# Eight PSUM banks for the node update, its bias in three batches, and fifty unread products on TensorE

## The reference

```python
features = x[src]                                             # 200000 x 64
Y = relu(concat([features, edge_attr], axis=1) @ M_W.T + M_b)
Z = segment_sum(Y, dst, num_segments=6250)
h = relu(concat([x, Z], axis=1) @ U_W.T + U_b)
out = layernorm(x + h)                                        # over 64 features, eps 1e-5
```

## Time and profile before

| | us |
|---|---|
| median of 3 runs (1639.28 to 1639.89) | 1639.65 |
| profiled execution, its own time | 1641.58 |
| its span, first to last instruction | 1639.7 |
| busy: TensorE, VectorE, GpSimd, ScalarE | 1596.5, 1332.8, 1223.9, 347.5 |

### The profile page before, as it was taken

How to read it: one execution, slowest core, us unless ns; L and a number is a source line. 1 busy time by engine, 2 the same in 40 slices (tenths; PEclk the granted TensorE clock), 3 DMA queues, 4 the chain that set the end, 5 groups by cost and what they waited for, 6 DMA issues and landing times.

```text
span 1639.7 us, 53864 instructions
## 1 busy us (share of the span) xinstructions
PE 1596.5 (97%) x18182; PEld 1542.8 (94%) x18182; DVE 1332.8 (81%) x1391; ACT 347.5 (21%) x661; POOL 1223.9 (75%) x1303
## 2 busy tenths in 40 slices
PE   5899999999999999999999999999999999999996
PEld 5899999999999999999999999999999999999995
DVE  6788887888887888888888788888788878878874
ACT  4431111212112112211211111211221211212111
POOL 6777777777777777777777777777777777777774
PEclk9999999999999999999999999999999999999998
DMA  8333332323333333333333333323333332323222
GB/s 176 71 72 72 70 79 65 80 64 79 66 79 65 76 75 71 73 66 79 69 74 72 71 73 72 74 69 73 71 72 78 67 78 65 80 65 78 66 59 47
DMA packets 177806, 120.89 MB, mean 74 GB/s; under 512 B 107140, under 2 KB 156018, under 8 KB 177528
## 3 DMA queue, kind: packets, MB, share of 16 engines
q0 software_dynamic: 40992, 42.04, 13.9%
q1 hardware_dynamic: 105754, 56.86, 13.4%
q10 hardware_dynamic: 30782, 18.51, 4.8%
HBM read 114.08 MB, written 3.20 MB: 72 GB/s over the span
## 4 chain that ended last, share of the span: by engine, by line
POOL 74%; issue 24%; PE 1%; DMA 0%; DVE 0%; POOLq 0%; ACT 0%; DVEq 0%
POOL gathered L427 74%; PE p_pick L1076 0%; DMA src_first<-in_src_dram 0%; PE p_edges_T L1076 0%; PE p_bc L1076 0%; DMA gathered<-Y_rows,src_last 0%; POOL Y L457 0%; PE p_pick L1069 0%; DVE Y L881 0%; POOLq L453 0%; PE p_edges_T L1069 0%; PE p_bc L1069 0%; PE p_bc L1032 0%; PE p_messages L1025 0%; DVE total L866 0%
## 5 line engine op out<-in xcount | busy, mean ns | idle before, releaser
L427 POOL DMA_INDIRECT gathered<-Y_rows,src_all x1238 | 1168.2, 944 | 377.6 <-issue 377.6
L1018 PE MATMUL p_pick<-Y_parts,onehot_src 128*128 128x192 bf16 x12397 | 1053.8, 246 | 7.8 <-DVE onehot_src L812 7.4
L1018 PEld LDWEIGHTS p_pick<-Y_parts,onehot_src 128*128 128x128 bf16 x12397 | 1027.6, 98 | 12.6 <-issue 10.5
L812 DVE TENSOR_TENSOR onehot_src<-p_dve,block_start 128x6272 bf16<-128x6272 int16 x253 | 860.5, 3422 | 6.5
L1025 PE MATMUL p_messages<-onehot,messages 128*64 128x72 f32 x3126 | 238.4, 230 | 4.9 <-ACT messages L568 4.9
L796 DVE TENSOR_TENSOR p_messages<-p_messages,gathered 128x512 f32<-128x512 f32 x191 | 133.3, 698 | 132.3 <-DMA gathered<-Y_rows,src_all 111.5
L1025 PEld LDWEIGHTS p_messages<-onehot,messages 128*64 128x64 f32 x3126 | 209.3, 137 | 29.1 <-ACT messages L568 5.9
L1001 PE MATMUL p_messages<-w_edges,edges_T 128*128 128x128 f32 x1564 | 213.3, 280 | 3.7 <-ACT edges_T L548 3.7
L1001 PEld LDWEIGHTS p_messages<-w_edges,edges_T 128*128 128x128 f32 x1564 | 190.9, 192 | 5.1 <-ACT edges_T L548 3.3
L548 ACT COPY edges_T<-p_edges_T 128x512 f32<-128x512 f32 x196 | 114.5, 584 | 379.8 <-PE p_edges_T L983 370.8
L562 ACT ACTIVATE match<-src_spread,minus_node 128x128 int16<-128x128 int32 x190 | 82.9, 436 | 526.8 <-issue 526.8
(11 more groups left out here) (119 smaller groups left out, 199.3 us busy)
## 6 DMA issues: line engine op xcount, KB each, us to landing
row_tile<-Y_rows SPq DMA_DIRECT2D x2560, 0.2 KB
edges<-in_edge_attr_dram SPq DMA_DIRECT2D x190, 192.0 KB
gathered<-Y_rows,src_all POOLq DMA_INDIRECT x1238
slow_tile<-Y_rows ACTq DMA_DIRECT2D x1152, 0.2 KB
edges<-in_edge_attr_dram SPq DMA_DIRECT2D x191, 64.0 KB
src_spread<-in_src_dram ACTq DMA_DIRECT2D x127, 64.0 KB
src_spread<-in_src_dram ACTq DMA_DIRECT2D x63, 128.0 KB
Y_rows<-Y SPq DMA_DIRECT2D x6, 256.0 KB
```

The costliest lines, as they stand in the source:

```text
L427: nc.gpsimd.indirect_dma_start(out=gathered[c % G][0:parts, j * D:(j + 1) * D], out_offset=None, in_=table, in_offset=bass.IndirectOffsetO ...
L812: nc.vector.tensor_tensor(onehot_src[k % SLOTS][:, :, :], sources.unsqueeze(1).to_broadcast([P, NW, P]), block_start[:, :, :], ALU.is_equa ...
L1018: last = nc.tensor.matmul(p_pick[k % 2][:, 0:3 * D], onehot_src[k % SLOTS][:, b, :], Y_parts[:, b, :], start=(b == 0), stop=(b == NW - 1))
```

## The change

- `p_update` lists all eight banks in a new order. To the four it adds the three `p_messages` banks and `p_dve`: half-groups 0 to 3 use `p_edges_T`, the two `p_pick` banks and the `p_messages` bank of chunk 193, half-groups 4 to 7 that of chunk 194, `p_bc`, `p_dve` and that of chunk 195.
- The bias products no longer stand one ahead of each half-group. `start_update` issues four ahead of chunk 195's window sums (behind four waits for the readers of their banks), four ahead of half-group 2, and five ahead of half-group 8, behind one wait for the fifth VectorE add. The wait for `s_h` ahead of each half-group from the fifth on is gone.
- The unread products: ahead of chunk 194's sums fifty for ten, ahead of chunk 195's sums eight for ten, ahead of half-group 0 eight for six. Since there are 49 blocks, the index wraps.

```diff
-        p_update = [p_edges_T, p_bc, p_pick[0], p_pick[1]]
+        p_update = [p_edges_T, p_pick[0], p_pick[1], p_messages[(NC + 1) % SLOTS], p_messages[(NC + 2) % SLOTS],
+                    p_bc, p_dve, p_messages[NC % SLOTS]]
...
                 for b in range(n):
-                    nc.tensor.matmul(p_bc[:, 0:3 * D], Y_parts[:, b, 0:P], Y_parts[:, b, :], start=True, stop=True)
+                    nc.tensor.matmul(p_bc[:, 0:3 * D], Y_parts[:, b % NW, 0:P], Y_parts[:, b % NW, :],
+                                     start=True, stop=True)
...
                 if c >= NC - 1:
-                    keep_clock(10)
+                    keep_clock(50 if c < NC else 8)
...
+                pe.wait_ge(s_u_parts, 1)
+                pe.wait_ge(s_chunk_added, NC - 1)
+                pe.wait_ge(s_pick_summed, len(picks))
+                pe.wait_ge(s_edges_T_copied, NC + 1)
+                start_update(0, 4)
                 windows(NC)
 
+            def start_update(k0, k1):
+
+                for k in range(k0, min(k1, len(half_groups))):
+                    b0, b1 = half_groups[k]
+                    nc.tensor.matmul(p_update[k % len(p_update)][:, 0:(b1 - b0) * 2 * D], ones_parts[:, :],
+                                     u_parts[:, 0:b1 - b0, :].rearrange("k b d -> k (b d)"), start=True, stop=False)
+
             def update():
-                pe.wait_ge(s_u_parts, 1)
-                pe.wait_ge(s_pick_summed, len(picks))
                 for k, (b0, b1) in enumerate(half_groups):
                     p = p_update[k % len(p_update)]
-                    if k >= len(p_update):
-                        pe.wait_ge(s_h, k - len(p_update) + 1)
-                    nc.tensor.matmul(p[:, 0:(b1 - b0) * 2 * D], ones_parts[:, :],
-                                     u_parts[:, 0:b1 - b0, :].rearrange("k b d -> k (b d)"), start=True, stop=False)
                     if k == 0:
-                        keep_clock(6)
+                        keep_clock(8)
                         pe.wait_ge(s_XZ, 1)
                         pe.wait_ge(s_chunk_added, NC + 1)
+                    if k == 2:
+
+                        start_update(4, 8)
+                    if k == 8:
+
+                        pe.wait_ge(s_h, len(half_groups) - 8)
+                        start_update(8, len(half_groups))
```

## The result

The median went from 1639.89 us (12 runs, 1639.28 to 1642.18) to 1636.70 us (12 runs, 1635.73 to 1637.52): ratio 0.9978, 95% interval 0.9970 to 0.9987, so 2.1 to 4.9 us, 3.2 between the medians. The profiled executions lie further apart: 1641.58 before, 1636.91 after, 4.67. Most of what follows is about why these two differences differ.

The account below looks back on a forecast made before the run. GpSimd's gather descriptors bind up to the last gather, TensorE the tail behind it. Gains 2.60 + (2.81 - 2.27) + 3 x (2.81 - 2.34) = 4.55 off the median 1639.65 give 1635.1 us; range 1634.2 to 1638.5.

Parts of the forecast that it names:

- The clock: TensorE in the tail: filling the 3.50 us of idleness keeps the granted clock at 1.00 from 1602 to the last half-group.
- C: Rival: TensorE's clock falls in the same place despite the filling, giving 1638.4 us; chance 0.10.
- E: Rival: TensorE's clock sinks in the update while cycling through more banks, giving 1645.8 us; chance 0.02.
- Rival D: Clock already low under the fifty products, which then outlast the release of chunk 194's sums at 1606.43: 1644.1 us; chance 0.05.
- The fifty cost nothing: Ahead of chunk 194's sums: fifty products end between 1605.99 and 1606.18, before the release at 1606.43, filling a hole.
- Shapes and batches: TensorE's tail: half-groups with no bias between load 0.89 apart; a four-bias batch takes 0.97, plus 0.20 for a shape switch.
- The third batch: Five biases ahead of half-group 8 take 1.4 at most, hidden behind VectorE with 0.2 to spare.
- Rival B: TensorE keeps the shape switch: half-groups 1.09 back to back, biases 0.31 each; 2.9 won, 1636.8 us; chance 0.12.
- VectorE binds from the third group: Second adds step by 2.27, then 2.34, instead of 2.81; last full group at 1625.04 against 1629.59.
- the last one of the sum: The 4.55 gain, read from a 1641.58 profile, was taken off the runs' median 1639.65, giving 1635.1.
- the term of 2.60: Gain by half-group 3's add, the fourth: 1615.75 instead of 1618.35.
- Who could be late next: GpSimd's two passes take 2.08 of a group's 2.34, and the DMA engines have room, so neither was expected to delay.

Follow-up runs that it names:

- e4: Changed kernel with 42 unread products instead of fifty ahead of chunk 194's sums: 1639.79 us, ratio 0.9979 to the kernel before.
- e11: Kernel before, no edit, third profile, a single execution: 1639.89 us, tail 31.81 us.
- e12: Kernel before, no edit, fourth profile, a single execution: 1642.77 us, tail 31.84 us.
- e8: Changed kernel, no edit, profiled again on a second chip: 1636.82 us, ratio 0.9978 to the kernel before.
- e10: Changed kernel, no edit, third profile, on a third chip: 1639.79 us, ratio 0.9978 to the kernel before.
- e5: Changed kernel with 42 unread products and without GpSimd's drain behind its last gather: 1639.86 us, ratio 1.0007 to the kernel before.
- e2: Changed kernel with ten unread products instead of fifty ahead of chunk 194's sums: 1642.19 us, ratio 0.9994 to the kernel before.
- e7: Changed kernel with 42 products, second and third bias batches moved, eight products ahead of half-group 0 and drain left out: 1640.69 us, ratio 1.0010 to before.
- e1: Kernel before, no edit, second profile, on a first chip: 1643.07 us, ratio 1.0002 to the kernel before.
- e9: Changed kernel with 42 products, moved biases, drain kept, first group's squares taken by ScalarE straight from h: 1639.28 us, ratio 0.9977 to the kernel before.

## Why the prediction was right or wrong

The time, 1636.7, lies in the range of 1634.2 to 1638.5 and the sign was right. The likeliest value, 1635.1, was 1.6 too low, and the gain of 4.55 two fifths above the measured 3.2. So the range held, and one term of the sum was too large.

**The clock: right in kind.** It stayed at 1.00 from 1602 to the last half-group with eight banks in turn; rivals C and E did not come about in the changed kernel's profiles. The Trainium skill ("TensorE: Matmul & The Clock Gate", section "A second HAM failure mode: psum-queue depth-cycling") tells of a kernel that goes through PSUM banks and whose clock swings, from short idle moments of TensorE between its groups. With eight banks this trace shows no swing, 1.00 from 1616 to 1618; but TensorE was busy for all of that stretch, so such moments were not put to the test. Rival D did not come about either: a product of the fifty takes 0.083 in the trace (4.17 for fifty). (In C's working four cold biases and eight cold products from 1607.58 end at 1611.2 by its own prices, not 1611.0; nothing hangs on it.)

**The fifty cost nothing: right in effect, for another reason.** They ended at 1606.83, not 1605.99 to 1606.18: their pace was right, but TensorE came to them at 1602.66 instead of 1601.83. They outlasted the release, which the prediction had as a sign of rival D and which came without it, and the 1st add was 0.27 later than forecast; the drain would have held that time anyway (e4).

**Shapes and batches: right.** 0.90 between neighbouring half-groups (0.89 forecast), 2.05 across the second batch (2.06), 0.97 for the first batch (0.97). The third batch, too, kept nobody waiting: half-group 8 loads 2.11 behind half-group 7, 1.22 more than a neighbour (1.4 at most forecast), and VectorE's adds have no bracket there. Rival B fell with the first of these.

**VectorE binds from the third group: right.** Its step was 2.25 where I had 2.34: two adds that need not wait start 0.29 apart, and the idle time before the second one, which I subtracted, did not hold that. Last full add: forecast 1625.04, measured 1624.93. That it is so close is partly luck: the fourth add came 0.27 late (1616.02 for 1615.75), and four shorter steps won that back. Between the two profiles the sum holds: 4.55 forecast, 33.41 - 28.83 = 4.58 in the tail.

**The step that failed** is the last one of the sum: "the runs' median is 1639.65, and the difference is taken off that". The 1.93 us between the profiled execution and the median were written down and then passed over. The changed kernel's profile lies only 0.21 above its median. What made the profiled execution long was the very stretch of low clock that the change removes, 6.8 us where the frequent execution has 3.4. So the term of 2.60, what was won by the fourth add, was sized by a rare execution: from the later profiles it is 10.46 - 9.34 = 1.1 (e11, e12 against e8), and VectorE's faster groups add 1.9 (21.70 - 10.46 against 18.64 - 9.34), together 3.0. Set against its own time, 1641.58 - 4.55 = 1637.03, the same sum would have met the profile after (1636.91) and come within 0.33 of the median; but that takes the equal G of the two profiles, which was luck.

**What was missing:** the drain. "Who could be late next" counted GpSimd's passes and not what stands ahead of the first one. In the frequent execution of before it already holds the first pass by 0.25 (mean at G + 9.00, pass at G + 9.25). In the changed kernel, with 50 or 42 products, it holds the pass by 1.1 to 1.6, and in three of four profiles (e4, e8, e10) VectorE then waits 0.27 to 0.35 for the first group's squares; in the first, whose adds came 0.4 later, it does not wait at all.

## What to carry to other kernels

A gain that is read off one profile belongs to that execution: set it against that execution's time, and if what is removed varies from execution to execution (here the clock), take a second profile before moving it to the median. Follow every engine that takes part in a tail back to its last instruction ahead of it, those that are not counted as busy included: here a drain took back 0.4 us of what was won (third group's second add at G + 11.92 in e4, 11.53 without the drain in e5). What an unread filling is worth hangs on what runs behind it: put alone into the kernel before it gave 1.0 by the medians, cut to ten products in the changed kernel it cost 2.4 (e2 against e4).

## What the runs showed of the hardware

- GpSimd's drain behind the last of the gathers ended 9.1 to 9.2 us after the start of that gather's descriptors in each of twelve profiles; between GpSimd's last pass and the end lay 5.1 us with it (e8), 8.4 and 8.5 without it (e5, e7).
- After 4.0 us of idleness TensorE's clock stayed low for 6.8 us in one execution (e1) and for 3.4 in another (e12); in e9's profile it fell although TensorE, by its busy time, had stood still for only 1.4 of the 6 us from 1600 on.
- Weight loads of one shape (128 columns, fp32) follow each other at 0.11 across a change of PSUM bank (eight in 0.90, from half-group 0 to 1); ahead of three-row products it was 1.09, 0.19 more (1611.87 to 1612.96).
